# Two setups rewritten and reordered, and products on zeros in TensorE's waits, in a two-layer attention and mixture kernel

## The reference, cut to what matters

```python
x = x + L0_xattn(layernorm(x), ctx)     # 16 heads of 64, low-rank parts, 77 keys, two key segments (73 + 4)
x = x + L0_ffn(layernorm(x))            # 8 experts of hidden 1024, top 2, and a shared one, silu
x = x + L1_xattn(layernorm(x), ctx)     # 8 heads of 32, biases, 77 keys
x = x + L1_ffn(layernorm(x))            # 8 experts of hidden 256, top 2, gelu

def L1_xattn(x, y):
    q, k, v = x @ Wq.T + bq, y @ Wk.T + bk, y @ Wv.T + bv      # split into 8 heads
    attn = softmax(q @ k.T / sqrt(32))
    return (attn @ v) @ Wo.T + bo
```

## Time and profile before

| | us |
|---|---|
| median of 3 runs (951.23 to 955.05) | 952.58 |
| the profiled execution's own time | 952.09 |
| its span, first to last instruction | 950.3 |
| TensorE busy | 870.8 (92%) |
| VectorE busy | 677.3 (71%) |
| ScalarE busy | 494.8 (52%) |
| GpSimd busy | 198.3 (21%) |
| mean granted TensorE clock | 0.962 |

### The profile page before, as it was taken

How to read it: one execution, slowest core, us unless ns; L and a number is a source line. 1 busy time by engine, 2 the same in 40 slices (tenths; PEclk the granted TensorE clock), 3 DMA queues, 4 the chain that set the end, 5 groups by cost and what they waited for, 6 DMA issues and landing times. The chain is left out here.

```text
span 950.3 us, 17912 instructions
## 1 busy us (share of the span) xinstructions
PE 870.8 (92%) x6265; PEld 800.6 (84%) x6265; DVE 677.3 (71%) x1316; ACT 494.8 (52%) x1001; POOL 198.3 (21%) x159
## 2 busy tenths in 40 slices
PE   8987999996979989999999999767998699999998
PEld 6775899995679989999999999636887478999997
DVE  3674899995784448888888889785876765665555
ACT  3643333332455566777777777224554444445553
POOL 7410333331014510333222232201222000000000
PEclk9979999998899999999999999977999899999999
DMA  8920000000303267677777777240000200010002
GB/s 299 298 95 0 2 0 1 1 1 7 138 26 126 95 203 267 223 225 236 228 234 222 214 227 235 55 145 1 0 1 0 90 23 1 24 40 27 0 1 89
DMA packets 47518, 97.44 MB, mean 103 GB/s; under 512 B 7298, under 2 KB 35172, under 8 KB 40932
## 3 DMA queue, kind: packets, MB, share of 16 engines
q1 hardware_dynamic: 38132, 85.23, 26.4%
q0 software_dynamic: 7152, 9.34, 4.9%
q10 hardware_dynamic: 2176, 2.10, 0.7%
HBM read 75.74 MB, written 20.91 MB: 102 GB/s over the span
## 5 line engine op out<-in xcount | busy, mean ns | idle before, releaser
L143 PE MATMUL e_ps_h<-e_xh,e_w1h 128*128 128x256 f32 (+1 forms) x496 | 141.9, 286 | 5.5 <-issue 5.5
L144 PE MATMUL e_ps_h<-e_xl,e_w1h 128*128 128x256 f32 (+1 forms) x496 | 139.4, 281 | 0.0
L145 PE MATMUL e_ps_h<-e_xh,e_w1l 128*128 128x256 f32 (+1 forms) x496 | 139.1, 281 | 0.0
L143 PE MATMUL e_ps_o<-e_w2h,e_hh 128*128 128x256 f32 x440 | 122.4, 278 | 0.0
L145 PE MATMUL e_ps_o<-e_w2h,e_hl 128*128 128x256 f32 x440 | 121.9, 277 | 0.0
L144 PE MATMUL e_ps_o<-e_w2l,e_hh 128*128 128x256 f32 x440 | 121.9, 277 | 0.0
L1890 ACT ACTIVATE e_hf<-e_ps_h,e_b1s 128x256 f32<-128x256 f32 (+1 forms) x248 | 98.1, 447 | 43.3 <-PE e_ps_h L145 38.3
L1770 POOL DMA_INDIRECT accumulated<-m_yo,m_token x39 | 74.0, 1897 | 198.8 <-ACT m_yo L1910 163.4
L982 POOL TENSOR_TENSOR at_pr<-at_pr,at_inv 128x1168 f32<-128x1168 f32 (+2 forms) x48 | 58.8, 1239 | 226.3 <-DVE at_inv L922 226.3
L143 PEld LDWEIGHTS e_ps_h<-e_xh,e_w1h 128*128 128x128 f32 x496 | 95.1, 192 | 5.7 <-issue 5.7
L144 PEld LDWEIGHTS e_ps_h<-e_xl,e_w1h 128*128 128x128 f32 x496 | 95.2, 192 | 0.0
(11 more groups left out here) (321 smaller groups left out, 2384.4 us busy)
## 6 DMA issues: line engine op xcount, KB each, us to landing
e_w1s<-in_m_w SPq DMA_DIRECT2D x24, 1024.0 KB
e_w2s<-in_m_w SPq DMA_DIRECT2D x24, 1024.0 KB, 7.2
slots_in<-zero SPq DMA_DIRECT2D x20, 258.0 KB, 8.1
e_xin<-slots_in SPq DMA_DIRECT2D x16, 258.0 KB, 4.8
as_wk<-in_a_wk SPq DMA_DIRECT2D x2, 1024.0 KB, 9.5
as_wv<-in_a_wv SPq DMA_DIRECT2D x2, 1024.0 KB, 11.9
X<-in_x SPq DMA_DIRECT2D x1, 2048.0 KB, 22.0
accumulated<-zero SPq DMA_DIRECT2D x8, 256.0 KB, 6.6
```

The lines of the kernel that those rows point to most:

```text
L143: nc.tensor.matmul(out, lh, rh, start=start, stop=False)
L144: nc.tensor.matmul(out, lh, rl, start=False, stop=False)
L145: return nc.tensor.matmul(out, ll, rh, start=False, stop=stop)
```

## The change

Four parts. (1) In the first setup two pieces move: on ScalarE `high_w(gi+2)` goes ahead of the copies `qh` and `oh`, and on VectorE the three bn_stats go from behind A_low to ahead of `low_diagonal(gi+1)`. (2) `attention_setup` is replaced by `second_setup`, for layer 1 alone. Both groups' keys and values go to psum buffers of their own; ScalarE now zeroes `kbd` (a broadcast copy of a zero), writes its diagonals (activation with bias), and copies the first row of `row`, for which it waits on `s_row`; VectorE keeps `vbd`, the subtractions, and does its additions into X only in the loop over B, two an item, and the last four behind it; the head mask goes to GpSimd. (3) TensorE does 14 products on zeros, fp32, 128x256, behind the last item of B. (4) In both attentions it does such products behind the transposes of x: 6 in step -1 of layer 0, 2 in that of layer 1, and 4 in step 0 of both.

```diff
+def warm(nc, g, out, times):
+    for _ in range(times):
+        nc.tensor.matmul(out, g.ident[:], g.zero[:, 0, 0:D], start=True, stop=True)
...
                 v.tensor_tensor(dst, src[:, gi, :], high, ALU.subtract).then_inc(s_ul, 1)
+            if gi >= 2:
+                for _ in range(3):
+                    if tiles < NT:
+                        prepare.tile_statistics(dve, tiles)
+                        tiles += 1
             if gi + 1 < G:
                 low_diagonal(gi + 1)
...
-            if gi >= 2:
-                for _ in range(3):
...
         for gi in range(G):
+            if gi + 2 < G:
+                high_w(gi + 2)
             for r, (src, dst) in enumerate(((wq, qh[:, gi % 2]), (wo, oh[:, gi]))):
...
-            if gi + 2 < G:
-                high_w(gi + 2)
             if gi + 1 < G:
                 high_diagonal(gi + 1)
...
-def attention_setup(nc, ctx, g, L, w, sem, prepare, before, early, after):
+def second_setup(nc, ctx, g, L, sem, before, early, after):
...
+    ps_kv = pb("ps_kv", [P, 2, G, 512])
+    ps_b = ps_kv[:, 0].rearrange("p q (a d) -> p q a d", d=D)
...
     def tensor(pe):
...
+        for gi in range(G):
+            for i, (weights, loaded) in enumerate(((wk, early.s_wk), (wv, early.s_wv))):
...
+                    last = nc.tensor.matmul(ps_kv[:, i, gi, 0:JB], weights[:, k, gi * P:(gi + 1) * P], c[:, k],
+                                            start=k == 0, stop=k == CK - 1)
             last.then_inc(s_kv, 1)
+        pe.wait_ge(early.s_wq, 64)
+        for a, (gi, b, k) in enumerate(a_items):
+            if (b, k) == (0, 0):
+                pe.wait_ge(s_bk, gi + 1)
+                for r in range(NB):
+                    wait(pe, s_ul, gi * NB + r - 1)
+                    nc.tensor.matmul(ps_u[0:1, r, 0:n], bq[:, gi:gi + 1], kbd[:, gi, r, :], start=True, stop=True).then_inc(s_u, 1)
+            wait(pe, s_alo, a - 1)
+            nc.tensor.matmul(ps_a[:, a % 2, 0:n], wq[:, gi, k * P:(k + 1) * P], kbd[:, gi, b, :], start=True, stop=True).then_inc(s_a, 1)
+        pe.wait_ge(s_bv, G)
+        pe.wait_ge(s_zh, 2)
...
+        warm(nc, g, ps_u[:, 0, 0:D], 14)
 
     def gpsimd(pool):
         stage_over(pool, after)
+        gp = nc.gpsimd
+        gp.memset(g.row[:].bitcast(FP), 0.0).then_inc(s_row, 1)
+        gp.memset(head0[:, 0:first], 1.0).then_inc(s_zh, 1)
+        gp.memset(head0[:, first:], 0.0).then_inc(s_zh, 1)
 
     def vector(dve):
         stage_over(dve, after)
-        if not L.lora:
-            first_head(nc.vector)
-            for zeros in (kbd, vbd):
-                nc.vector.memset(zeros[:], 0.0).then_inc(s_zero, 1)
...
+        v.memset(vbd[:], 0.0).then_inc(s_zv, 1)
+        dve.wait_ge(s_zv, 1)
+        dve.wait_ge(early.s_wv, 32)
+        for gi in range(G):
             dve.wait_ge(s_kv, gi + 1)
             for hh in range(hp):
...
+                last = v.tensor_scalar(vbd[rows, :, at:at + KEYS], kv(rows, gi, 1), bv[rows, gi:gi + 1], None, ALU.add)
+            last.then_inc(s_bv, 1)
+        for a, (gi, b, k) in enumerate(a_items):
+            if (b, k) == (0, 0):
+                for r in range(NB):
+                    dve.wait_ge(s_uh, gi * NB + r + 1)
+                    v.tensor_tensor(g.row[LOW:SPLIT, r, keys(gi)], ps_u[0:1, r, 0:n], g.row[0:1, r, keys(gi)], ALU.subtract).then_inc(s_ul, 1)
+            dve.wait_ge(s_ahi, a + 1)
+            v.tensor_tensor(g.Al[L.n][:, b, k, keys(gi)], ps_a[:, a % 2, 0:n], g.Ah[L.n][:, b, k, keys(gi)], ALU.subtract).then_inc(s_alo, 1)
+        tiles = 0
+        for i, (b, c0, nch) in enumerate(b_items):
+            for _ in range(2):
+                before.add(dve, tiles)
+                tiles += 1
             dve.wait_ge(s_bhi, i + 1)
...
+        for t in range(tiles, NT):
+            before.add(dve, t)
+        before.statistics(dve)
+        deviation.dve(dve)
 
     def scalar(act):
         stage_over(act, after)
+        a_ = nc.scalar
+        a_.copy(kbd[:].rearrange("p g b j -> p (g b j)"), g.zero[:, 0, 0:1].to_broadcast([P, G * NB * n])).then_inc(s_zk, 1)
+        act.wait_ge(s_zk, 1)
+        act.wait_ge(early.s_wk, 32)
         for gi in range(G):
+            act.wait_ge(s_kv, gi + 1)
+            for hh in range(hp):
+                rows, at = slice(dh * hh, dh * (hh + 1)), hh * KEYS
+                last = a_.activation(kbd[rows, gi, :, at:at + KEYS], kv(rows, gi, 0), ACT.Identity, bias=bk[rows, gi:gi + 1])
+            last.then_inc(s_bk, 1)
+        act.wait_ge(s_row, 1)
+        for a, (gi, b, k) in enumerate(a_items):
+            if (b, k) == (0, 0):
+                for r in range(NB):
+                    act.wait_ge(s_u, gi * NB + r + 1)
+                    a_.copy(g.row[0:1, r, keys(gi)], ps_u[0:1, r, 0:n]).then_inc(s_uh, 1)
+            act.wait_ge(s_a, a + 1)
+            a_.copy(g.Ah[L.n][:, b, k, keys(gi)], ps_a[:, a % 2, 0:n]).then_inc(s_ahi, 1)
...
                 if not static or t + 2 < NT:
                     transpose_x(t + 2, q)
+                if static and t <= 0:
+                    warm(nc, g, ps_o[:, 0:D], 4 if t == 0 else 6 if L.lora else 2)
                 if not static or t >= 1:
```

More of the change, by code:

```diff
@@ L556, in attention_setup @@
-    b_items = [(b, ch, min(2, L.chunks - ch)) for b in range(NB) for ch in range(0, L.chunks, 2)]
-    def first_head(eng):
-        keys = L.segments[0][1]
-        eng.memset(head0[:, 0:keys], 1.0).then_inc(s_zero, 1)
-        eng.memset(head0[:, keys:], 0.0).then_inc(s_zero, 1)
-    def sync(sp):
-        groups = () if early else ((loads, s_w), (loads_k, s_wk), (loads_v, s_wv), (loads_lq, s_lq), (loads_q, s_wq))
-        for group, loaded in groups:
-            for dst, src in group:
-                sp.dma_start(dst[:], src).then_inc(loaded, 16)
-        if prepare:
-            prepare.load(sp)
-        if prepare:
-            prepare.zero_slots(sp)
-        if before:
-            before.sync(sp)
@@ L735, in vector @@
-        for i, (b, ch, nch) in enumerate(b_items):
-            dve.wait_ge(s_bhi, i + 1)
-            nc.vector.tensor_tensor(g.Bl[L.n][:, b, ch:ch + nch, :], ps_b[:, i % 2, 0:nch, :],
-                                    g.Bh[L.n][:, b, ch:ch + nch, :], ALU.subtract).then_inc(s_blo, 1)
-            for _ in range(nch):
-                add_tile()
-        while added[0] < NT:
-            add_tile()
-        if before:
-            before.statistics(dve)
-            deviation.dve(dve)
+                rows, at = slice(dh * hh, dh * (hh + 1)), hh * KEYS + off[gi]
@@ L748, in scalar @@
         stage_over(act, after)
-        if L.lora:
-            act.wait_ge(s_al, 1)
-            for i in range(2):
-                act.wait_ge(s_lk, i + 1)
-                nc.scalar.activation(low[:, i], ps_u[0:RANK, i, 0:NB * KEYS].rearrange("p (b j) -> p b j", b=NB),
-                                     ACT.Copy, scale=al[:, 1 + i:2 + i]).then_inc(s_lk_sb, 1)
-        for gi in range(G):
-            for j, (b, k0) in enumerate(a_items):
-                a = gi * len(a_items) + j
-                act.wait_ge(s_a, a + 1)
-                nc.scalar.copy(g.Ah[L.n][:, b, k0:k0 + KA, gi * n:(gi + 1) * n], half_a(a)).then_inc(s_ahi, 1)
-            if prepare and gi == G - 2:
-                deviation.act(act)
@@ L763, in scalar @@
+        act.wait_ge(s_row, 1)
[6 more added lines that the diff above has]
+            a_.copy(g.Ah[L.n][:, b, k, keys(gi)], ps_a[:, a % 2, 0:n]).then_inc(s_ahi, 1)
+        for i, (b, c0, nch) in enumerate(b_items):
             act.wait_ge(s_b, i + 1)
-            nc.scalar.copy(g.Bh[L.n][:, b, ch:ch + nch, :], ps_b[:, i % 2, 0:nch, :]).then_inc(s_bhi, 1)
@@ L765, in scalar @@
-        if before:
-            deviation.act(act)
-    return Stage(sync, tensor, gpsimd, vector, scalar, (s_blo, len(b_items)))
+            a_.copy(g.Bh[L.n][:, b, c0:c0 + nch, :], ps_b[:, i % 2, 0:nch, :]).then_inc(s_bhi, 1)
+        deviation.act(act)
+    return Stage(before.sync, tensor, gpsimd, vector, scalar, (s_blo, len(b_items)))
 def attention(nc, ctx, g, L, sem, after):
@@ L2080, in attend @@
                 else:
-                    first = attention_setup(nc, setup, g, L, weights(L), sem, prepare, before, early, after)
+                    first = second_setup(nc, setup, g, L, sem, before, early, after)
             return first, attention(nc, own, g, L, sem, first)
```

185 lines of the change are left out of this document (18 added, 167 removed).

## The result

| | before | after |
|---|---|---|
| first comparison, median (lowest to highest) | 952.1 (951.2 to 955.1), 4 runs | 937.9 (935.4 to 940.6), 4 runs |
| ratio, 95% interval | | 0.9846 [0.9806, 0.9887] |
| the same kernel in two later groups, ratio | | 0.9896 [0.9846, 0.9945]; 0.9911 [0.9876, 0.9945] |
| executions of all groups (their number): mean and its standard error | 951.6 ± 0.3 (105) | 941.7 ± 0.8 (21) |
| profiled execution, span in it | 952.09, 950.3 | 940.64, 938.7 |

What follows compares the result with a forecast made beforehand. TensorE was taken as busiest in the first setup, VectorE in the second, with the granted clock mattering around them. -4.3 - 1.5 - 2.7 - 2.0 = -10.5 us gave a forecast of 941.8 us, range 937.5 to 947.5.

Steps and rivals of the forecast that it cites:

- A: First setup, two pieces reordered: 3.3 us of waits for as_wl go, and 1.0 of 3.2 for ql; -4.3 us.
- B: First attention, 6 and 4 products on zeros: second scores run at full clock; -1.5 us, bounds 0 and -1.6.
- D: 14 zeros at second setup's end, 2 and 4 in second attention: clock held for its first scores; -2.0 us.
- C: Second setup rewritten: VectorE's work moves to ScalarE and GpSimd, so it ends earlier; -2.7 us, bounds -1.6 and -3.4.
- The upper bound: First setup: -7.3 us if the shorter last gap also keeps the clock up, some 3 us more; none taken.
- the bound of -3.4: Second setup: the largest gain allowed for its rewriting, where -2.7 us was forecast.
- nearer to the full gain, as the gap shrinks from 8.1 us: Second attention's start: 1 to 3 us idle remain behind the zeros, yet -2.0 is taken, between 0 and -2.6.
- 2 (clock not held): Both attentions: clock falls in the gap behind the zeros, B and D give 0; 945.1 us, chance 0.12.
- 1: Second setup: the wait for row, or ScalarE itself, becomes the bound and C gives 0; 944.3 us, chance 0.13.
- 3: First setup: another link is next and only the last round's 1.0 us comes; 944.9 us, chance 0.06.
- 4: Zeros leave the clock low and delay ready work in the attentions, ending slower; 953.2 us, chance 0.05.
- Half a per cent as what can be told: Whole kernel: half a per cent is about what a measurement can tell from no change, 947.8 and 957.3 us.

Runs made afterwards that it cites:

- reorder_only: The kernel before with both pieces of the first setup moved and nothing else changed; median 947.60 us, ratio 0.9953.
- filled: row_dve_22 plus fp32 zeros in the first setup, 5 ahead of the last group's A products and 4 behind the last b product; 934.19 us, ratio 0.983.
- row_dve_22: The kernel after with row zeroed by VectorE instead of GpSimd and 22 instead of 14 zeros at the second setup's end; 936.75 and 937.08 us.
- setup_22: The kernel after with 22 instead of 14 products on zeros at the second setup's end; mean 943.0 ± 1.5 us.
- setup_only: The kernel after with only its rewritten second setup: first setup's order of before, no added zeros; 946.66 us, ratio 0.9969.
- no_zeros: The kernel after without any of the added products on zeros; median 939.1 us.
- no_zeros_2: The kernel after without any of the added products on zeros, measured a second time in a later group; median 943.96 us.
- after_3: The kernel after, unchanged, measured again as the common measure of a later group; median 942.19 us.

## Why the prediction was right and wrong

The forecast of 941.8 missed the first comparison, 937.9 (937.4 by its ratio), and met the mean of 21 executions, 941.7 ± 0.8. The first is chance in part: four runs that lay low. The second is luck in part: of the four terms A and B were right, and the step that failed is D, the clock held over to the second attention (2.0 forecast, 0.6 to 0.8 measured), while C was mis-sized the other way (2.7 forecast, 3.5 measured). By the profiles the four come to 4.0 + 1.4 + 3.5 + 0.8 = 9.7, where 10.5 was forecast and the totals have 9.9.

- **A, -4.3: right in size, the working half right.** Loop -4.0 in the profiles, -4.3 ± 1.1 in the totals of reorder_only. The wait for `as_wl` went, that for `ql` fell from 3.2 to 2.4 (to 2.2 was said). The text took both moves as needed for the 3.3 us of `as_wl`; by one profile each, `high_w`'s move alone gives 2.5, and the statistics' move alone the whole. The upper bound (the low clock behind the last gap, 3 us) was rightly left out: the clock was still low behind the gap, 2.4 us or more, in every profile but that of filled. When it is filled, 1 to 2 us of the 3 come out before x.
- **B, -1.5: right in its place, unseen in the total.** The six zeros took 2.76 us (0.46 each, not 0.56) and left 0.66 us idle, cost nothing, and the second set ran at 1.00 in all 12 profiles that have them. The premise that the clock is low there without them held in 5 of 8. On average over profiles it is 1.4. In totals it could not be seen.
- **C, -2.7: too small.** -3.5 in the profiles, -4.5 ± 1.1 in the totals, past the bound of -3.4. The chain was as described, with ScalarE waiting 1.82 us for `row`. The mis-sized terms: the old stage was taken as 34.2 from one profile, and the five have 34.6 on average; A_low ended 14.8 us into the stage in the undisturbed profiles, where 15.0 to 15.7 was taken, and the additions with B_low took 15.7, where 15.9 was taken. The 0.7 us added for a stretch of low clock were true of three profiles in ten.
- **D, -2.0: failed.** The step "nearer to the full gain, as the gap shrinks from 8.1 us". The zeros were priced at 0.56 to 0.93 each, and took 0.444; so they ended 3.3 us ahead of x and not 0 to 2. The row that was at hand, 3.25 us of idle time followed by a low clock, was a warning of what such a gap can do. The 14 gave 0.6 and D as a whole 0.8, and the first scores stayed at 0.50 to 0.56 in all six profiles that have them; with the gap filled, another 1.7.
- **Rivals.** 2 (clock not held) is half true: for D, not for B. 1 and 3 fell: C gave 3.5 and not 0, A 4.0 and not 1.0. 4 fell too: the six and the 14 ended ahead of the work they stood before.
- **Half a per cent as what can be told:** too optimistic. With a spread of 3.4 us between executions, four runs leave 1.7 us of standard error, and the four first runs gave 14 us for a change of 9.9.

## What to carry to other kernels

Before pricing a stall by its named releaser, follow that releaser's own queue back: here one engine's late, movable work (three bn_stats) lay behind both waits, and in the one profile of it moving that work alone gave all. Here zeros meant to keep TensorE's clock paid fully only where they reached the next real work; price them at full clock, and count the idle time that is left behind them. Where low-clock stretches move a kernel by several us from run to run, compare stretches between fixed points in several profiles.

## What the runs showed of the hardware

- Products on zeros, fp32, 128x256: 0.44 us each in a long row (9.66 us for 22), 0.46 and 0.49 in short ones (2.76 us for 6, 2.43 for 5).
- Zeroing 128x1232 fp32 took 1.08 us on VectorE, 1.20 on ScalarE (a copy) and 1.72 on GpSimd.
- A biased Identity of ScalarE over 32x154 took 0.39 us, eight in a row 3.15, with no table load ahead of them: 596.94 + 1.20 to 598.18.
- A gap of TensorE of 2.4 or 3.3 us was followed by a granted clock of 0.50 in after (60.00:64.00, 633.60:637.36); a hole of 0.35 and one of 0.92 us was not (row_dve_22, setup_22). A gap's length alone doesn't decide it: the 3.25 us ahead of the first attention's second scores, with no zeros there, were followed by a set at 1.00 in three profiles (setup_only, no_zeros, no_zeros_2) and by one at a low clock in five.
- The first attention's first scores took 3.55 us at 1.00 in after and 6.01 at 0.55 in after_3, the same kernel: where a low stretch falls changes from execution to execution.

```profile
81.25:87.26 6.01, 6.01 (x19) 4.90 (x20) 0.00 (x0) 0.00 (x0) 0.00 (x0) 0.55 0.00 0
```
